# MLP weight preparation one piece per attention step, a reordered setup, and a rest block of 128 rows

## The reference, cut to what matters

```python
mod = (silu(c) @ wmod).reshape(1, 6, 1, 256)          # c (1, 256), wmod (256, 1536)
sa, ca, ga, sb, cb, gb = six slices of mod            # ga, gb: sign * max(|.|, 0.25)
h = layernorm(x) * (1 + ca) + sa
# retention: 16 heads of 16, causal mask with decay, rotary sines and cosines
q, k, v, g = rms(h, retn_norm_w) @ (q_w, k_w, v_w, g_w)
o = rms(((rot(q) rot(k)^T) * mask / denom) @ v)
x2 = h + (silu(g) * o) @ out_w
y = x2 + gelu(rms(x2, final_norm_w) @ fc1_w + fc1_b) @ fc2_w + fc2_b   # fc1 256x1024
x = x + ga * y
h = layernorm(x) * (1 + cb) + sb
# 16 experts of 176, top 4 of a softmax router; shared MLP of 704 rows
x = x + gb * (shared(h) * sigmoid(h @ gate_vec) + sum_k weight_k * expert_k(h))
```

## Time and profile before

| | us |
|---|---|
| median of 3 runs | 606.09 |
| lowest, highest | 603.9, 609.25 |
| profiled execution, first to last instruction (span) | 601.3 |

### The profile page before, as it was taken

One profiled execution on the slowest core, in us unless ns is written; L12 is line 12 of the kernel. 1 busy time (PEld: TensorE's weight loads), 2 busy tenths in 40 slices (PEclk: granted clock), 3 DMA queues, 4 the chain that ended last, 5 costly groups with the idle time before them and its releaser, 6 DMA issues.

```text
span 601.3 us, 14769 instructions
## 1 busy us (share of the span) xinstructions
PE 546.0 (91%) x4215; PEld 475.7 (79%) x4216; DVE 462.8 (77%) x1178; ACT 294.2 (49%) x728; POOL 328.2 (55%) x402
## 2 busy tenths in 40 slices
PE   3879889999998999998789999986999999999995
PEld 1557677888877988887666778865999999999983
DVE  3688989898753499898886878866777677777776
ACT  3355554665555664644234355544444444444471
POOL 2356777878765455635377778800354444454430
PEclk9999999999999999999899999997999999999997
DMA  8522121221700421211348967647744444344968
GB/s 297 201 58 78 45 89 46 89 87 44 223 2 1 117 86 54 88 38 46 117 140 300 385 195 229 206 121 244 231 128 137 123 124 130 122 140 133 317 229 278
DMA packets 68697, 85.95 MB, mean 143 GB/s; under 512 B 10688, under 2 KB 59712, under 8 KB 68640
## 3 DMA queue, kind: packets, MB, share of 16 engines
q1 hardware_dynamic: 58480, 63.34, 34.1%
q0 software_dynamic: 6864, 18.88, 8.6%
q10 hardware_dynamic: 3296, 3.03, 1.6%
HBM read 53.72 MB, written 29.40 MB: 138 GB/s over the span
## 4 chain that ended last, share of the span: by engine, by line
PE 37%; DVE 7%; DMA 3%; issue 3%; ACT 1%; SPq 0%; POOL 0%; DVEq 0%; POOLq 0%; ACTq 0%
PE bank L2302 13%; PE bank L1988 6%; PE bank L2320 5%; PE bank L2006 4%; PE bank L2322 3%; PE bank L2286 3%; PE bank L2312 3%; DMA results<-yb,xe 2%; DMA wgu_lo<-results 1%; DVE s_a_lo L1845 1%; ACT s_a_hi L1710 1%; DVE hid L1836 1%; PE bank L2347 1%; DVE sh L1855 0%; DVE wdt L2226 0%
## 5 line engine op out<-in xcount | busy, mean ns | idle before, releaser
L2163 POOL DMA_INDIRECT results<-yb,xe x79 | 75.8, 959 | 111.2 <-DVE yb L2251 107.3
L1649 POOL DMA_INDIRECT dispatched<-rows,slot x64 | 66.4, 1038 | 18.8 <-issue 12.5
L2302 PE MATMUL bank<-wgu_hi,xT_hi 128*128 x158 | 59.1, 374 | 6.0 <-DVE xT_lo L2232 6.0
L2245 DVE TENSOR_TENSOR e_hT_lo<-bank,e_hT_hi 128x256 fp32r<-128x256 f32 x79 | 33.6, 425 | 33.1 <-ACT e_hT_hi L2196 31.3
L2302 PE MATMUL bank<-wgu_lo,xT_hi 128*128 x158 | 51.8, 328 | 0.0
L2302 PE MATMUL bank<-wgu_hi,xT_lo 128*128 x158 | 51.8, 328 | 0.0
L2196 ACT CAST e_hT_hi<-bank 128x256 fp32r<-128x256 f32 x79 | 29.4, 373 | 41.6 <-PE bank L2312 41.5
L2191 ACT ACTIVATE e_sg<-bank 128x176 f32<-128x176 f32 x79 | 25.1, 318 | 48.8 <-PE bank L2302 48.8
L758 DVE TENSOR_TENSOR probs<-bank,causal 128x512 f32<-128x512 f32 x64 | 39.7, 683 | 12.0 <-PE bank L948 12.0
L613 POOL TENSOR_TENSOR orms<-omse,neghalf 128x16 f32<-128x16 f32 x16 | 47.1, 2945 | 0.3
L1988 PE MATMUL bank<-h3T_hi,wsg_hi 128*128 128x512 f32 x88 | 36.4, 413 | 4.0 <-PEq L149 1.7
(11 more groups left out here) (250 smaller groups left out, 1898.0 us busy)
## 6 DMA issues: line engine op xcount, KB each, us to landing
xe<-dispatched SPq DMA_DIRECT2D x79, 128.5 KB, 2.2
trig<-t_trig SPq DMA_DIRECT2D x16, 512.0 KB, 3.7
wgu_raw<-expert_gu SPq DMA_DIRECT2D x16, 352.0 KB, 7.6
xt<-L_attn_x SPq DMA_DIRECT2D x32, 128.0 KB, 3.3
wgu_hi<-results SPq DMA_DIRECT2D x8, 512.0 KB, 7.7
wgu_lo<-results SPq DMA_DIRECT2D x8, 512.0 KB, 8.9
dispatched<-fill SPq DMA_DIRECT2D x4, 520.0 KB
x_rows<-h_all SPq DMA_DIRECT2D x16, 128.0 KB, 2.0
```

The source lines that it names most:

```text
L1649: pool.indirect_dma_start(out=dram["dispatched"], out_offset=bass.IndirectOffsetOnAxis(ap=slot[:, k, t:t + 1], axis=0), in_=rows[:, t, :], ...
L2163: pool.indirect_dma_start(out=dram["results"], out_offset=bass.IndirectOffsetOnAxis(ap=xe[r][:, E:E + 1].bitcast(INT), axis=0), in_=yb[:, ...
L2245: nc.vector.tensor_tensor(hT[1][:, q, :], hT_bank[p][:, 0:2 * P], hT[0][:, q, :].bitcast(F32), ALU.subtract).then_inc(S["h_lo"], 1)
L2302: mm = nc.tensor.matmul(gu_bank[p][:, 0:GU], xT[xn_][:, p, k, :], wgu[wn][:, k, e, :], start=(k == 0 and i == 0), stop=(k == KB - 1 and i ...
```

## The change

One piece of MLP weight work stands in each attention body instead of two in each of six, on VectorE now between `split_hT` and the masks. The later gate moves behind the attention. ScalarE's second-layer casts move to bodies 9 to 12, one each. `ident` gets a semaphore of its own; the waits for all tables move to the first readers; modulation 1 moves behind tile 0 together with 2, and its copy to body 2; x tile 1 is loaded earlier. The loop of bodies 10 to 15 is written out. The rest block's second matmul reads 128 rows, with weights that were there already.

```diff
     def pipeline(eng, body):
-        for t in range(HEAD):
+        for t in range(NT):
             body(t, t % 2, lambda lag, t=t: t - lag >= 0)
-        with eng.Fori(HEAD // 2, NT // 2) as j:
-            for p in range(2):
-                body(j * 2 + p, p, lambda lag: True)
         body(NT, NT % 2, lambda lag: lag >= 1)
+    GATED2, LOW1, HIGH2, LOW2 = (8, 9, 10, 11), (4, 5, 6, 7), (8, 9, 10, 11), (12, 13, 14, 15)
...                                                       # sync
+        load_x(1, 1)
         load_trig(0, 0)
         for c in (1, 2):
             sp.dma_start(wmod[...]).then_inc(S[f"wmod_in{c}"], 16)
-        load_x(1, 1)
...                                                       # scalar
-        load_table(*TABLES[0])
+        load_table(ident, "t_ident", "ident_in")
...
-        act.wait_ge(S["tables"], ALL_TABLES)
         def high_weights(t):
             if t == 1:
+                keep_mod(1)
                 act.wait_ge(S["wo_in"], 16)
...
-            if t in (4, 5):
-                for n in (2 * t - 8, 2 * t - 7):
+            if t in HIGH2:
+                n = HIGH2.index(t)
...
+            if t == 2:
+                act.wait_ge(S["tables"], ALL_TABLES)
             if live(2): evacuate_k(t - 2, p)
...
-            if isinstance(t, int) and t == 1:
-                keep_mod(1)
...                                                       # vector
         def low_weights(t):
+            if t == 2:
+                dve.wait_ge(S["tables"], ALL_TABLES)
+                low_out()
-            if t == 0:
+            if t == 3:
                 dve.wait_ge(S["mod_sb"], 2)
                 gate(modb[:, 2, :], modb[:, 2, :])
-            if t in (2, 3):  # two gated pieces each
-            if t in (4, 5):  # two low first-layer pieces each
-            if t in (6, 7):  # two low second-layer pieces each
+            if t in GATED2:  # one gated piece
+            if t in LOW1:    # one low first-layer piece
+            if t in LOW2:    # one low second-layer piece
+        def later_gate():
+            dve.wait_ge(S["mod_sb"], 3)
+            gate(modb[:, 5, :], gb[:, :])
+            nc.vector.tensor_scalar(modb[:, 4, :], modb[:, 4, :], 1.0, None, ALU.add).then_inc(S["gates"], 1)
+            dve.wait_ge(S["gates"], 3)
...
-                dve.wait_ge(S["tables"], ALL_TABLES)
...
             if live(1): split_hT(t - 1, q)
+            if t < NT:
+                low_weights(t)
             if live(2):
                 for b in MASKS:
                     mask(t - 2, b)
-            if isinstance(t, int) and t >= 1:
-                low_weights(t - 1)
             if live(1): rope(t - 1, q)
...
         mlp.ahead.split(2)
+        later_gate()
         mlp.ahead.split(3)
...                                                       # tensor
         modulation(0)
-        pe.wait_ge(S["wmod_in1"], 16)
-        modulation(1)
-        pe.wait_ge(S["tables"], ALL_TABLES)
+        pe.wait_ge(S["ident_in"], 16)
...
             if number == 1:
-                pe.wait_ge(S["wmod_in2"], 16)
-                modulation(2)
+                for c in (1, 2):
+                    pe.wait_ge(S[f"wmod_in{c}"], 16)
+                    modulation(c)
...                                                       # shared MLP, second product
-                for an, wn, m in ((0, 0, P), (0, 1, P), (1, 0, P)) if b < LAST else ((0, 0, P), (0, 1, HROWS)):
-                    mm = nc.tensor.matmul(dst, a1[an][0:m, b % RING, i * P:i * P + P], wsd[wn][0:m, b, :],
+                for an, wn in ((0, 0), (0, 1), (1, 0)) if b < LAST else ((0, 0), (0, 1)):
+                    mm = nc.tensor.matmul(dst, a1[an][:, b % RING, i * P:i * P + P], wsd[wn][:, b, :],
```

More of the change, by code:

```diff
@@ L396, in sync @@
                 load_trig(j * 2 + p, p)
-    TABLES = [(ident, "t_ident"), (norm, "t_norm"), (smask, "t_smask"), (causal, "t_causal"), (parity, "t_parity")]
+    TABLES = [(parity, "t_parity"), (causal, "t_causal"), (norm, "t_norm"), (smask, "t_smask")]
     ALL_TABLES, PREP = 16 * len(TABLES), 4
@@ L404, in scalar, with load_table @@
     def scalar(act, mlp):
-        def load_table(dst, name):
-            act.dma_start(dst[tuple([slice(None)] * len(dst.shape))], io[name]).then_inc(S["tables"], 16)
+        def load_table(dst, name, landed="tables"):
+            act.dma_start(dst[tuple([slice(None)] * len(dst.shape))], io[name]).then_inc(S[landed], 16)
         def keep_mod(c):
@@ L412, in scalar @@
         act.dma_start(wmod[:, :, 0:2 * E], wmod_rows[:, :, 0:2 * E]).then_inc(S["wmod_in0"], 16)
-        load_table(*TABLES[0])
+        load_table(ident, "t_ident", "ident_in")
         act.wait_ge(S["vecs"], 32)
         nc.scalar.activation(scol[:, :], ccol[:, :], ACT.Silu).then_inc(S["silu_c"], 1)
-        for table in TABLES[1:]:
+        for table in TABLES:
             load_table(*table)
@@ L437, in high_weights @@
                 nc.scalar.activation(wf1[0][:, k, :], w1_32[:, k, :], ACT.Identity, scale=fw[:, k:k + 1]).then_inc(S["w1_hi"], 1)
-            if t in (4, 5):
-                for n in (2 * t - 8, 2 * t - 7):
-                    act.wait_ge(S["w2_ga"], n + 1)
-                    nc.scalar.copy(wf2[0][:, part2(n), :], w2_32[:, part2(n), :]).then_inc(S["w2_hi"], 1)
+            if t in HIGH2:
+                n = HIGH2.index(t)
+                act.wait_ge(S["w2_ga"], n + 1)
+                nc.scalar.copy(wf2[0][:, part2(n), :], w2_32[:, part2(n), :]).then_inc(S["w2_hi"], 1)
         def square_h(t, p):
@@ L702, in low_weights @@
-            if t in (2, 3):
-                dve.wait_ge(S["w2_in"], 16)
[L704 to L707, removed]
-            if t in (4, 5):
[L709 to L713, removed]
@@ L714, in low_weights @@
-            if t in (6, 7):
[L715 to L718, removed]
-                dve.wait_ge(S["w1_lo"], 4)
+            if t in GATED2:
+                n = GATED2.index(t)
+                dve.wait_ge(S["w2_in"], 16)
+                dve.wait_ge(S["gates"], 1)
+                nc.vector.tensor_tensor(w2_32[:, part2(n), :], w2_32[:, part2(n), :], modb[:, 2, :].unsqueeze(1).broadcast_to([P, QUART2, E]),
+                                        ALU.mult).then_inc(S["w2_ga"], 1)
@@ new lines, in low_weights @@
+            if t in LOW1:
+                n = LOW1.index(t)
+                k, cols = part1(n)
+                dve.wait_ge(S["w1_hi"], k + 1)
+                nc.vector.scalar_tensor_tensor(wf1[1][:, k, cols], w1_32[:, k, cols], fw[:, k:k + 1], wf1[0][:, k, cols].bitcast(F32),
+                                               ALU.mult, ALU.subtract).then_inc(S["w1_lo"], 1)
+            if t == LOW1[-1]:
+                dve.wait_ge(S["w1_lo"], 4)
+            if t in LOW2:
+                n = LOW2.index(t)
+                dve.wait_ge(S["w2_hi"], n + 1)
+                nc.vector.tensor_tensor(wf2[1][:, part2(n), :], w2_32[:, part2(n), :], wf2[0][:, part2(n), :].bitcast(F32), ALU.subtract).then_inc(S["w2_lo"], 1)
@@ L824, in body @@
                 low_projections(1)
-                dve.wait_ge(S["tables"], ALL_TABLES)
                 dve.wait_ge(S["prep"], PREP)
-            if isinstance(t, int) and t == 2:
-                low_out()
             if live(3): gate_o(t - 3, q)
```

3 lines of the change are left out of this document (1 added, 2 removed).

## The result

| | before | after |
|---|---|---|
| median of 4 runs, us | 605.74 | 595.46 |
| lowest, highest | 603.9, 609.25 | 594.54, 597.85 |
| profiled execution: span | 601.3 | 594.1 |
| ratio, 95% interval | | 0.9845 (0.9813 to 0.9878) |

The changed kernel is faster by 1.55%, and the interval leaves no doubt about the sign. The forecast was 598.4, its range 594.0 to 603.5. The profiled execution after took 595.94 in all, 1.8 more than its span. Ratios leave out executions more than 1.5% above the fastest of the same kernel, medians don't, which matters for experiments 7 and 8 and for one execution of the kernel before beside experiments 1 to 4 (2341.65).

The account below looks back on a forecast made before the run. Bare attention steps were taken as bound by TensorE, weight steps by a ring through VectorE. Attention -5.4 and rest block -2.3 gave -7.7 on span 601.3, so 593.6; with the 4.8 difference kept, 598.4, range 594 to 603.5.

Parts of the forecast that it names:

- The ring and the hole: Attention steps: work between mask and rope is paid in full; VectorE's 0.60 idle ahead of masks hides pieces, 0.2 total.
- ScalarE's casts in bodies 9 to 12: Attention: each 0.64 cast exceeds ScalarE's 0.29 idle, the other 0.35 delays q and scores; 1.4 for four steps.
- The double cast of body 4: Attention body 4: first-layer ScalarE cast, twice as wide, about 1.3, formerly covered; charged 1.0.
- Setup: Kernel start to r2 (rope start, 41.61 before): TensorE later by 2.4 (-0.75, clock +1.3, modulation +1.88); r2 41.6, no change.
- The later gate: End of attention, between two VectorE subtractions for the MLP: 1.8 of work where VectorE idles; cost 0, at most 1.8.
- Rest block: Shared MLP's rest block: 128-row matmuls 0.12 apart; TensorE saves 5.4, of which 2.3 arrives; bounds 0 and -5.4.
- rival 4: Rest block worth nothing: spacing has another cause than 64 rows, or VectorE's chain swallows all; 2.3 more, 600.7; chance 0.08.
- From span to time: Whole kernel: span 593.6, with the same 4.8 difference to the median kept, gives 598.4.
- Rival 1: Setup: the clock is up in time; 1.3 less, 597.1; chance 0.15.
- rival 2: Attention: holes are not free, pieces take 0.87 beside GpSimd, 3.2 instead of 0.2; 601.4; chance 0.15.
- rival 3: Attention: work ahead of masks is itself on the ring, 12 steps grow by 0.87; 11.4 more, 609.8; chance 0.07.
- Rival 5: Rest block: TensorE's saving arrives in full, 5.4 instead of 2.3; 595.3; chance 0.07.

Follow-up runs that it names:

- experiment 7: Changed kernel with 64 rows again in the rest block of the first three groups, 128 in the last, second chip: 618.05, 0.9866, inconclusive.
- experiment 8: Changed kernel with modulation 1 in TensorE's gap before tile 0's projections and the later gate behind the last MLP subtraction, second chip: 608.54, 0.9809.
- experiment 1: The changed kernel again, no edit, first chip: 595.46, 0.9831 against the kernel before.
- experiment 2: Changed kernel with the weight pieces, still one a body, behind the masks instead of ahead of them: 606.86, 1.0019 against the kernel before.
- experiment 3: Changed kernel with the rest block's 64-row second matmul put back: 597.71, 0.9867 against the kernel before.
- experiment 4: Changed kernel with modulation 1 put into TensorE's gap, behind the transposes of h and ahead of tile 0's projections: 592.44, 0.9798.
- experiment 11: Changed kernel with modulation 1 in TensorE's gap and the later gate behind the last MLP subtraction, third chip: 592.3, 0.979.
- experiment 10: Changed kernel with 64 rows in the rest block of the first three groups, 128 in the last alone, third chip: 596.93, 0.9865.
- experiment 6: The kernel before, no edit, profiled a third time, on the second chip: 621.3, span 619.5.

## Why the prediction was right, step by step

The outcome was the forecast's: faster by over 1%, the time in the range, 3 us below the predicted value. The span was forecast at 593.6 and came out at 594.1, partly by luck, because errors cancelled: up to r15 the change gave 7.5 instead of 5.4, while the later gate and the stretch behind it cost 1.0 and the shared MLP's first group 2.2, where the forecast had nothing.

- **The ring and the hole.** Right, and shown by experiment 2: the same twelve pieces behind the masks cost 11.4 us more (11.6 between r2 and r15). The term for pieces (0.2) holds; in bodies 8 to 11 steps are 8.89 and 8.90. The steps of bodies 6 and 7 are 9.08 and 8.97, which no experiment explains. The loop written out is not tested by itself; bare steps before are 8.93, steps with a piece 8.90, so it can hardly be worth more than the 0.03 a step.
- **ScalarE's casts in bodies 9 to 12**, charged 1.4. Too dear. Each cast stands in a body whose step takes 8.9: they cost nothing. The delay of 0.35 for q, which the step assumed to arrive at the scores, doesn't; the bound of 0 was the right end.
- **The double cast of body 4**, charged 1.0: r2 to r3 is 9.27, 0.35 above the mean of the twelve others (8.92). Together the casts were 2.4 in the sum and are some 0.4 in the trace; 13 steps take 116.3 instead of 118.7.
- **Setup.** The projections start at 16.78, earlier than the 17.3 forecast. The clock is the setup's most wrongly sized term: 1.3 for seven matmuls, measured 5.25 - 2.87 = 2.4 for twelve. The step carried over 3 us from the moved modulation; here the level stays at the lower one for 5.3 us of matmuls back to back, while in experiment 2, same setup, it rose after six. In the other runs of this setup it rose after ten to twelve. So the usual case is the 2.2 that the prediction gave for all twelve, and it varies from run to run. Modulation: 1.79 measured, 1.88 forecast. TensorE enters step 2 2.9 later (2.4 forecast), r1 is 32.38 (31.9), r2 41.93 (41.6). VectorE does wait for a load of x (1.38, before 22.45), which the prediction listed as a bad sign; but the kernel before waits 1.69 for the same load (before 23.14), and it costs nothing, since the next thing that TensorE needs of it waits for ScalarE until 28.48.
- **The later gate**, charged 0 with a bound of 1.8: 0.8 by the first residual (0.4 of it is seen as TensorE's wait at 186.08). The idle of the earlier trace rows was there, but beside four GpSimd multiplications (180.82 to 184.23) the gate took 3.3, and the next subtraction came late. A place five subtractions later cures it (experiment 11).
- **Rest block.** Spacing 0.12 as forecast, and 2.3 in the time (experiment 3) as forecast. Inside it the last block gave 1.4 (1.46) and the first three 1.25 (0.89): the sum took the cast's wait of 0.89 and left out the wait of 0.23 at 394.37, which it had named; both are gone (experiment 10). The prediction read the row rule of the Trainium skill's page TensorE: Matmul & The Clock Gate ("Step-by-step: what each phase is for") as a rule on the spacing. The rule is about the load, and the loads agree with it (0.18 and 0.19), so it doesn't speak for rival 4. And 0.25 of idle loader stands only ahead of the first 64-row load; the later ones start 0.31 apart and take 0.18, which leaves 0.13.
- **Not foreseen:** 2.2 us in the first group of the shared MLP. In this profile the lower clock level falls on its first nine matmuls, ScalarE's silu starts 2.7 after the stage's first matmul instead of 1.66, and what follows waits. The eight kernels with the change on the first and third chip all take 46.2 to 46.9 for the stretch that took 44.8. But the clock does not do it in the same way in all of them: in experiments 4 and 11 the first twelve matmuls stand 0.23 apart, as in the profile of before, and the lower level starts only with the second block. And it is not the change's alone: in experiment 6, the kernel before, the first block falls to the lower level with its fifth matmul.

```profile
285.17 0.51 PE L1988 MATMUL bank<-h3T_lo,wsg_hi 128*128 128x512 f32 x1
285.47 0.63 PE L1988 MATMUL bank<-h3T_hi,wsg_lo 128*128 128x512 f32 x1
285.90 0.63 PE L1988 MATMUL bank<-h3T_hi,wsg_hi 128*128 128x512 f32 x1
```

Up to VectorE's fifth product, from its first matmul, the stage takes 35.3, 35.8 and 36.2 in the three profiles of the kernel before, and 36.7 to 37.5 in the eleven with the change. So up to 1.0 of the 2.2 is luck of the first profile. That the rest comes from the change is likely from these numbers, but not shown; why the level falls where it does is open. It could not be read from the trace of before.

- **From span to time.** The forecast kept a difference of 4.8 between span and median; it was 1.4 after. These 3.4, less the 0.5 by which the span was missed, are the 3 us between 598.4 and 595.5. That the profile of before was a quick one could be told (4.8 below the median, 2.6 below the lowest run); its true surcharge of 1.8 could not.

Rival 1 (clock up in time) was the opposite of what happened; rival 2 failed at a piece of 0.68; rivals 3 and 4 fell with experiments 2 and 3. Rival 5 failed too: of TensorE's 5.4 about 2.6 arrived (74.12 less 71.50), the last block and the waits for TensorE in the last group, not the rest.

## What to carry to other kernels

Work that is off the bound costs by its place in the dependence ring: here the same twelve instructions cost next to nothing ahead of a wait and 11 us behind it, so look for the engine's own idle time ahead of its latest releaser, and count its whole idle time in a step, not one hole. When matmuls at the front of a kernel seem to be in the way, ask whether they fill a gap that would otherwise leave the next ones at the lower clock; of the three places tried here, inside the gap was the best. Convert a predicted span into a time by the surcharge of the profiled run, and treat the profile's distance from the median as luck of that run.

## What the runs showed of the hardware

- A VectorE product or subtraction of 128x512 takes 0.68 beside GpSimd's power and 1.15 where GpSimd's elementwise product (0.62) runs beside it; a TENSOR_SCALAR of 128x256 takes 0.83 beside GpSimd's multiplications of 128x256 and 0.29 with GpSimd idle.
- After 2.3 us of idle, preceded by 4.6 to 5.0 with only two short transposes between, twelve matmuls ran 0.43 apart to the end in some runs, to the tenth or eleventh in others and to the sixth in one; with four matmuls in the gap they ran 0.23 apart from the second, third or fourth on.
- fp32r weight loads alternating between 64 and 128 rows start 0.31 apart, of 128 rows alone 0.12; each load takes 0.18 or 0.19.
- One chip of three took some 12 us more for the kernel before; in two profiles there, most of the excess stands in the first group of the shared MLP, where routing runs, with attention nearly unchanged.
